# The parts of a PSUM tile issued at their own places, or all at the last one's: dense work laid between attention scores on TensorE

## The reference

```
L0: xn = group_norm(x); q, k, v = qkv_w xn + qkv_b; h = softmax(q^T k / sqrt(32)) v, 8 heads of 32
    x = x + proj_w h + proj_b
L1: e = x; a = group_norm(e) * g + b + pos_emb
    s1 = silu(conv1x1(a)); s2 = silu(conv3x3(s1)); w = sigmoid(conv1x1(s2))     # 256 -> 32 -> 32 -> 1 channels
    sh = group_norm(a) * g + b
    standard = 8-head attention of sh (heads of 32); multi = two attentions of width 128, q from a * w, k and v from sh
    f = silu([standard, multi] ff_w1 + b) ff_w2 + b; final = group_norm(f out_w + out_b)
    x = final + e
L2: as L0 with 8 heads, result xn + proj_w h + proj_b
L3: one head of width 256: x = x + out_w softmax(q^T k / sqrt(256)) v + out_b
```

## Time and profile before

| What | Value |
|---|---|
| three runs | 5116.31, 5100.68, 5101.54 us |
| the profiled execution | 5115.33 us, its span 5113.5 us |
| TensorE (PE) busy | 4808.0 us, 94% of the span |
| VectorE (DVE) busy | 3027.6 us, 59% |
| ScalarE (ACT) busy | 2410.8 us, 47% |
| GpSimd (POOL) busy | 3031.0 us, 59% |
| granted TensorE clock, mean | 0.963 |

### The profile page before, as it was taken

How to read it: one execution, slowest core, us unless ns; L and a number is a source line. 1 busy time by engine, 2 the same in 40 slices (tenths; PEclk the granted TensorE clock), 3 DMA queues, 4 the chain that set the end, 5 groups by cost and what they waited for, 6 DMA issues and landing times. The chain is left out here.

```text
span 5113.5 us, 62532 instructions
## 1 busy us (share of the span) xinstructions
PE 4808.0 (94%) x21736; PEld 2227.6 (44%) x21736; DVE 3027.6 (59%) x5400; ACT 2410.8 (47%) x4321; POOL 3031.0 (59%) x1719
## 2 busy tenths in 40 slices
PE   7789999999999999999999999999999999999887
PEld 3235334553335533464334633346334553335434
DVE  6455677366773667636675467645677366773462
ACT  3352555435563456624555245542565435553251
POOL 3472677447873478635776357763677437864361
PEclk8899999999999999999999999999999999999999
DMA  3111212021210221102220112201122021210110
GB/s 90 31 35 45 56 43 56 21 56 46 58 35 21 73 47 44 38 28 65 57 47 20 42 50 61 56 8 48 50 55 57 17 60 47 49 44 11 29 38 13
DMA packets 105141, 223.39 MB, mean 44 GB/s; under 512 B 31616, under 2 KB 33920, under 8 KB 104704
## 3 DMA queue, kind: packets, MB, share of 16 engines
q1 hardware_dynamic: 104832, 219.39, 16.7%
HBM read 56.47 MB, written 8.39 MB: 13 GB/s over the span
## 5 line engine op out<-in xcount | busy, mean ns | idle before, releaser
L908 ACT ACTIVATE probs<-bank 128x512 f32<-128x512 f32 x3456 | 1929.5, 599 | 2308.2 <-PE bank L564 2273.4
L1011 DVE TENSOR_REDUCE max_cols<-bank 128x1 f32<-128x512 f32 x3456 | 2186.6, 680 | 1214.2 <-PE bank L564 1207.4
L1261 POOL TENSOR_TENSOR probs_added<-probs_added,probs 128x1024 f32<-128x1024 f32 x838 | 1960.4, 2377 | 55.4 <-ACT probs L908 55.0
L564 PE MATMUL bank<-q_stack,k_stack 97*128 97x512 f32 (+1 forms) x3584 | 1664.6, 519 | 77.2 <-DVE max_cols L1011 30.6
L564 PE MATMUL bank<-probs,v_tokens 128*32 128x512 f32 (+1 forms) x7168 | 1350.9, 625 | 10.3 <-ACT probs L908 8.8
L564 PEld LDWEIGHTS bank<-q_stack,k_stack 97*128 97x128 f32 (+1 forms) x3584 | 659.8, 193 | 767.6 <-issue 394.4
L1261 POOL TENSOR_TENSOR probs_added<-probs 128x1024 f32<-128x1024 f32 x192 | 454.0, 2369 | 839.3 <-ACT probs L908 836.8
L564 PE MATMUL bank<-act,weight_stream 128*128 128x512 f32 x1792 | 930.6, 619 | 16.5 <-issue 6.9
L1248 POOL TENSOR_TENSOR probs_added<-probs_added,probs 128x512 f32<-128x512 f32 x288 | 368.2, 1278 | 625.9 <-ACT probs L908 624.7
L564 PEld LDWEIGHTS bank<-probs,v_tokens 128*32 128x32 f32 (+1 forms) x7168 | 316.3, 121 | 411.5 <-issue 287.2
L564 PEld LDWEIGHTS bank<-act,weight_stream 128*128 128x128 f32 x1792 | 326.1, 194 | 337.2 <-issue 299.3
(11 more groups left out here) (84 smaller groups left out, 2868.2 us busy)
## 6 DMA issues: line engine op xcount, KB each, us to landing
k_stack<-high_parts SPq DMA_DIRECT2D x384, 128.0 KB, 2.4
q_stack<-high_parts SPq DMA_DIRECT2D x768, 64.0 KB, 2.0
weight_stream<-stream_dram SPq DMA_DIRECT2D x32, 768.0 KB, 4.3
k_stack<-low_parts SPq DMA_DIRECT2D x192, 128.0 KB, 2.4
q_stack<-low_parts SPq DMA_DIRECT2D x384, 64.0 KB, 2.0
act<-x_dram SPq DMA_DIRECT2D x8, 1024.0 KB, 6.4
act<-pos_dram SPq DMA_DIRECT2D x8, 1024.0 KB, 5.4
weight_stream<-stream_dram SPq DMA_DIRECT2D x16, 512.0 KB, 3.8
```

Of the source, the lines that this page charges most:

```text
L564: return nc.tensor.matmul(dst, lhsT, rhs, start=start, stop=stop, **kw)
L908: act.activation(PR[:, PLACE[m], j, :], bank[:, :], ACT.Exp, scale=att.scale).then_inc(reading(key), 1)
L1011: dve.tensor_reduce(cols[:, kh, j, qt:qt + 1], bank[:, :], AX.X, ALU.max).then_inc(reading(key), 1)
L1261: pool.tensor_tensor(ADD[:, js, :], one, two, ALU.add).then_inc(p_added, 1)
```

## The change

`tile()` gives all parts of a tile the time of the last part. The ` out` event keeps its time, and so do ` one`, ` mix`, ` low`, `stats` and everything else in the lists. Where a tile had parts in several units, with scores and attention work between them, they are now issued one behind the other in the unit of the last. Tiles with one part stay as they are.

```diff
 def tile(name, i, parts, at, step=1.0, out=1.5):
 
-    return [(at + k * step, name, (i, k)) for k in range(parts)] + [(at + (parts - 1) * step + out, name + " out", i)]
+
+    last = at + (parts - 1) * step
+    return [(last, name, (i, k)) for k in range(parts)] + [(last + out, name + " out", i)]
```

## The result

| | before | after |
|---|---|---|
| median (range) of four runs each | 5106.91 us (5100.68 to 5116.31) | 5157.72 us (5149.18 to 5164.95) |
| profiled execution, its span | 5115.33, 5113.5 | 5164.95, 5163.1 |
| mean granted clock | 0.963 | 0.967 |

The ratio is 1.0096, with a 95% interval from 1.0076 to 1.0116. The change makes the kernel slower by 1%, some 50 us. It was forecast to be some 20 us faster, with a chance of 0.16 for slower, and the time lies above the range given (up to 5115).

A forecast was written before the change was run, and what follows sets the result against it. PE was taken as the bound where dense parts stand, VectorE's maxima elsewhere. From 5101.5 us, -10.5 - 9.0 - 3.9 + 1.4 + 1.4 = -20.6 gave 5080.9, plus 2 for the clock 5083; 8-in-10 range 5058 to 5115.

The forecast's parts named there:

- Grouping itself costs nothing for 128x128 tiles: On PE, two scores then two parts take 2.18 us, 1.09 a pair as when alternating; cost put at 0.
- sa2, -9.0 and +1.4: Beside attention 2: grouping three parts saves 0.64 us a tile, 9.0 us in all; new waits cost 1.4 us.
- proj, -10.5: Beside attentions 2 and 1: Q starts 0.85 us earlier, so PE's waits for the projection's add go, 10.5 us.
- Rival (a): VectorE sets the length, so proj's and sa2's gains are mostly handed on; about -8 us, 5097; chance 0.22.
- ffo, -3.9: Third ffo tile: its first part's 0.56 us wait for the last ff1 mix goes, 3.9 us in 7 turns.
- ff1, q, k, v: Nothing to gain; bursts and lagging ScalarE cost ff1 0.2 us a turn, 1.4 in all; q, k, v 0.
- Fewer held banks can't save more: In the stretch with ff1, PE idles only 0.71 us, so holding banks for less time gains nothing.
- The clock, +2: A turn 2.9 us shorter meets the clock's falls at other points; 2 us added for a turn changing kind.
- Rival (b): Holes at units 6 to 9 and 54 to 57: PE waits for maxima, clock falls; 5113 or 5135; chance 0.18.
- Rival (c): Two to three banks more often free shorten waits and keep the clock up; 3 us a turn more, 5062; chance 0.10.
- What would show it: Marks for right or wrong: waits at lines 1173 and 1201, sa2 group 3.1 us, pair lengths, clock, maxima's waits.

The follow-up runs named there:

- g_ff: The kernel before with only the parts of ff1 and ffo grouped at the last part's place; ratio 0.9994 to the kernel before.
- ff_pairs: The changed kernel with ff1's four parts issued in two groups of two, 2 units apart; ratio 1.0035 to the kernel before.
- best_b: g_projsa2 with the third ffo tile grouped as well; ratio 0.9935 to the kernel before.
- g_rest: The kernel before with all tiles but ff1 and ffo grouped (proj, sa1, sa2, sa3, q, k, v); ratio 1.0019 to the kernel before.
- g_projsa2: The kernel before with only the proj and sa2 tiles grouped; ratio 0.9936 to the kernel before, 5079.3 us.
- held_early: The changed kernel, but each tile with several parts takes its bank at its first part's old place; ratio 1.0293 to the kernel before.

## Why the prediction was wrong

Point by point, in the order of its steps:

- **Grouping itself costs nothing for 128x128 tiles.** Right, as far as shown, for the ff parts themselves: with short exps g_ff's stretch is within 0.8 us of the interleaved one. (The 256-column parts of v take 0.10 us more together.) Wrong as the price of the edit, since it looked at two scores and two parts, a dose that costs little (ff_pairs, 0.6 us).
- **sa2, -9.0 and +1.4.** Right. The timeline after has each tile whole:

```profile
2604.57 0.51 PE L566 MATMUL bank<-high_parts 32*128 32x512 f32 x4
2605.01 2.76 PE L566 MATMUL bank<-act,weights 96*32 96x512 f32 x6
2607.70 0.98 PE L566 MATMUL bank<-q_stack,k_stack 97*128 97x512 f32 x3
2608.99 2.74 PE L566 MATMUL bank<-act,weights 96*32 96x512 f32 x6 [0.31 <-ACT probs L910]
```

  From Q to the score behind the first tile it takes 3.13 us, forecast some 3.1; the parts are 0.9 apart. The saving is 0.9 us a turn, 6.2 in all, against 7.6 net. What took the rest isn't VectorE's maxima but exp: the 0.31 us in brackets. The 0.9 saved and these 0.3 are 1.2 of the 1.3 us that four alternations cost at 0.32. That agrees with the rule cited from the Trainium skill (TensorEngine Tiling (Array Packing), Tiling Modes, Key Properties), that a switch of the mode drains TensorE.
- **proj, -10.5.** Right in mechanism, and low: -0.91 us at each of 14 places, 12.7. The second Q stands in the turn above at

```profile
2545.75 0.51 PE L566 MATMUL bank<-high_parts 32*128 32x512 f32 x4
2546.18 0.50 PE L566 MATMUL bank<-q_stack,k_stack 97*128 97x512 f32 x1
2546.52 1.88 PE L566 MATMUL bank<-act,weight_stream 128*128 128x512 f32 x4
```

  3.67 us behind the start of its attention (2542.08), 4.55 before (2520.58 less 2516.03): 0.88 earlier, forecast 0.85. Two whole tiles follow it, and no wait for the add is left. Rival (a), the gains handed on, is wrong for both.
- **ffo, -3.9.** Wrong in its size: best_b takes the wait away and gains 0.1 us of 0.56 in a turn, so about 0.7 in all. A wait of 0.43 us for exp took over at the next score. The step held that nothing would, "since PE is at its floor around it".
- **ff1, q, k, v: "+1.4 (0 to 7)", and for q, k, v 0.** This step failed, and it is nearly the whole error: +28.7 us for ff1 with ffo and +40 for v, q and k, against 1.4. (sa1, +3, had no term at all.) The prediction said that "spare banks and the burst behind it absorb this". It named the mechanism ("after a burst four scores come at once, and ScalarE [...] lags a little") and priced it by ScalarE's busy share, 24.87 of 45.70 us. That share says nothing about a queue that gets its work in heaps. A sum of the heap would have warned, though not given the size: four exps at 0.5 us, a tanh and a +1 at 0.55 each are 3.2 us, against PE's cycle of 2.93, which is 0.3 for each of four bursts where 1.0 was measured. And the waits for exp were in the list, with 35.6 us in 75 pieces, and should have stood beside the maxima as an engine near its limit. For v, q and k the step compared the number of parts in a cycle, which is the same, and not their order in it: they now come in bursts of two, with scores one behind the other between them. That this order costs the 40 us is shown (g_rest against g_projsa2); by which wait is not.
- **"Fewer held banks can't save more."** It was put at nothing because PE had little to wait for beside ff1, and the other pairs weren't asked. held_early shows that without the shorter hold the change would lose 150 us, only 0.9 a turn of it beside ff1 and most in the pairs beside 2 and 1. For the order of before the sentence is neither borne out nor refuted.
- **The clock, +2.** A turn came out 8 us longer and not 2.9 shorter, so the term as given wasn't put to the test. As a possible term it was too small: shifts of about 4 us in a turn changed the time at half clock from 378 us to 255 and 266, worth 24 to 32 us.
- **Rival (b), bursts leave holes.** The right sign, the wrong wait. Its number for one fall a turn (5113) is 45 us under the result. It had PE stand for the maxima and the clock fall for it. The waits for the maxima are unchanged (83.8 against 82.4), the clock beside ff1 is at 1.00, the mean clock is higher than before, and the waits for exp doubled. New falls came beside it, in three turns beside attention 1 (135.91 us at 0.95 above; 3.1 to 6.0 us more than in the other turns, 12 in all) and in four at unit 42 beside 2, where (b) had looked for one at 54 to 57. Other falls went, so these aren't what the 50 us are made of. The rule from the Trainium skill that the prediction put beside (b) (TensorE: Matmul & The Clock Gate, "A second HAM failure mode: psum-queue depth-cycling") did not decide beside ff1: PE cycles through its banks with short waits at full clock (49.12 us at 1.00). The prediction's reading that the trace shows falls only where waits of 1 us and more come in each cycle was wrong. In the kernel before, beside attention 2, the clock fell after 6.8 us in which PE was busy for 6.46, with one listed wait of 0.3:

```profile
2589.60:2596.40 6.80, 6.46 (x40) 2.14 (x42) 4.36 (x8) 5.56 (x11) 0.00 (x0) 1.00 0.00 0
2596.40:2599.80 3.40, 3.40 (x15) 0.95 (x15) 2.26 (x5) 2.54 (x6) 1.87 (x1) 0.50 0.00 0
```

- **Rival (c), more free banks.** The banks do count, as held_early shows, but its 3 us a turn on top didn't show: the pairs beside 2 and 1 of g_projsa2, at full clock, are at 144.8 and 128.4, near the forecast's own 145.3 and 128.6.
- **What would show it.** Of the marks given for "wrong", the maxima's waits (+1.4 us), the clock beside ff1 and the pairs with 3 and m stayed still; the mark that would have told, waits for exp, wasn't on the list. Pairs with 3 and m unchanged, 1173 at 0, 1201 near 1 (1.6 us), sa2's 3.1: these came true. The pair beside 0 at 160 (165.5), beside 2 at 145.3 (149.9) and beside 1 at 128.6 (131.6) failed, by ff1, v, q and k and by the falls beside 1.

Left open: the 0.8 us of ff1's loss that short exps don't give back; by what wait q, k and v lose their 40 us, the larger part of the loss, and how much of it is their late place; and what brings the clock down beside attention 1 in turns 3 to 5 and at unit 42 beside 2.

## What to carry to other kernels

An engine that follows another through a small pool of buffers is better fed evenly: look at the backlog that a burst leaves (how many items then come at what spacing, against the follower's time for one, and how many buffers lie between), and don't price it by the follower's busy share. Here such a sum gives the warning, a quarter of the size; a run with shorter items at the follower gives the rest. Before grouping or spreading work, sort the edit by tile: here the same move gained 0.9 us at a place where it removed a wait or a change of tile size and lost up to 4.1 us in a stretch where it only made bursts, and the best kernel makes it for two kinds of tile of eight (0.9936). When a local change is measured through the whole time on a kernel whose clock falls now and then, compare the same stretch between the same instructions first; a control that only adds time tells how much of the rest is the clock.

## What the runs showed of the hardware that I had not expected

- Adding about 30 us of matmuls (before_padded) left the time where it was (1.0012, interval 0.9992 to 1.0031), because the time at half clock went from 378 to 266 us. In this kernel the place of the clock's falls is sensitive to some four us in a turn of 614.
- PE can lose time to another engine without an idle row: in g_ff's stretch 4.1 us were lost, but the listed waits are 3.2 us against 0.6 before; the rest is in what the profile counts as busy.
- A tile's bank taken one to four units earlier, with the order of all matmuls unchanged, cost some 100 us (held_early 1.0293, after 1.0096), though it is one bank of eight, or two for a short while.
